# A vision layer with mixture of experts: expert loop written out, and expert results added into the normed rows by the indirect store

## The reference

```python
h = tok(x)                                   # patches @ W + b, class token, + pos_emb
h = layernorm(h + attention(h))              # 12 heads of 16, causal softmax
h = layernorm(h + moe(h))
```

```python
logits = xf @ Wg
scores, idx = top_k(logits, 2);  weights = softmax(scores)
for k in range(2):
    # position of each token in the list of its k-th expert, dropped from `capacity` on
    xg = xpad[buf]                            # (E, capacity, D)
    h = xg @ W1;  act = h[..., :H] * silu(h[..., H:])      # H = 512
    ye = act @ W2
    out = out.at[buf].add(w_buf * ye)         # dropped slots add nothing
```

## Time and profile before

| | |
|---|---|
| median of 3 runs | 2559.57 us (2555.77 to 2575.37) |
| the profiled execution | 2548.11 us |
| its span, first to last instruction | 2546.3 us |
| TensorE busy | 2192.3 us, 86% |
| DVE busy | 1640.0 us, 64% |
| POOL busy | 1389.2 us, 55% |
| ACT busy | 1105.0 us, 43% |
| mean granted TensorE clock | 0.938 |
| HBM read, written | 167.29 MB, 144.66 MB |

### The profile page before, as it was taken

The page is one execution under the profiler, slowest core; times in us unless marked ns, Lnnn a source line. Parts: engine busy times, 40 slices in busy tenths (PEclk is TensorE's granted clock), DMA queues, the critical chain, the costliest instruction groups (busy, mean ns, idle before and its releaser), DMA issues. The chain is left out here.

```text
span 2546.3 us, 50467 instructions
## 1 busy us (share of the span) xinstructions
PE 2192.3 (86%) x14772; PEld 2108.3 (83%) x14772; DVE 1640.0 (64%) x4491; ACT 1105.0 (43%) x2880; POOL 1389.2 (55%) x2562
## 2 busy tenths in 40 slices
PE   4798899999999999999989379989998999899900
PEld 3687799988989898988988379989998999899800
DVE  4366577777767677776767456656665666566556
ACT  2243344444444444444434145545454545454424
POOL 3234566665656666675756645444554545454456
PEclk8799899999999999999999789999999999999955
DMA  6889854545454454545443031101111110102187
GB/s 200 238 251 289 251 147 122 152 106 137 112 130 123 121 137 99 139 102 129 111 102 70 17 117 55 54 23 55 47 31 48 30 47 25 52 24 69 37 317 294
DMA packets 195651, 293.43 MB, mean 115 GB/s; under 512 B 43155, under 2 KB 146536, under 8 KB 190144
## 3 DMA queue, kind: packets, MB, share of 16 engines
q1 hardware_dynamic: 110480, 179.47, 25.1%
q10 hardware_dynamic: 57136, 99.73, 13.6%
q0 software_dynamic: 27904, 12.54, 2.1%
HBM read 167.29 MB, written 144.66 MB: 123 GB/s over the span
## 5 line engine op out<-in xcount | busy, mean ns | idle before, releaser
L653 PE MATMUL Y<-p,vp 128*102 128x198 f32 x1536 | 411.9, 353 | 15.9 <-POOL p L429 7.4
L140 POOL TENSOR_TENSOR e_word<-e_word 1x1 f32<-1x1 f32 x400 | 148.5, 371 | 435.2 <-DVE yout L1241 386.6
L442 POOL DMA_INDIRECT expert_lists<-pay,slot x256 | 283.1, 1106 | 58.9 <-issue 58.9
L1150 PE MATMUL Y<-w,a_hi 128*128 128x384 f32 x960 | 305.9, 357 | 10.1 <-DVE a_lo L1246 10.1
L1256 DVE TENSOR_TENSOR a<-UP,gate 128x384 f32<-128x384 f32 x320 | 178.3, 557 | 206.2 <-ACT gate L1197 205.9
L407 POOL TENSOR_TENSOR x_lo<-x,x_hi 128x396 fp32r<-128x396 f32 x192 | 212.1, 1107 | 177.8 <-ACT x_hi L462 175.9
L498 ACT ACTIVATE p<-ST 128x396 f32<-128x396 f32 x384 | 191.1, 498 | 269.2 <-PE ST L632 251.1
L1197 ACT ACTIVATE gate<-GT 128x384 f32<-128x384 f32 x320 | 157.5, 492 | 299.2 <-PE UP L1134 298.9
L1068 POOL DMA_INDIRECT expert_results<-yout,target x240 | 240.0, 1000 | 58.0 <-issue 58.0
L140 POOL TENSOR_TENSOR word_p<-word_p 1x1 f32<-1x1 f32 x416 | 90.8, 218 | 327.7 <-ACT p L500 316.3
L655 PEld LDWEIGHTS Y<-p,vp 70*102 70x102 f32 x1536 | 264.8, 173 | 1.4
(11 more groups left out here) (192 smaller groups left out, 6634.7 us busy)
## 6 DMA issues: line engine op xcount, KB each, us to landing
x<-in_xt ACTq DMA_DIRECT2D x30, 1188.0 KB
q<-qk_features SPq DMA_DIRECT2D x384, 74.2 KB, 6.4
k<-qk_features SPq DMA_DIRECT2D x192, 148.5 KB, 7.3
expert_lists<-blank ACTq DMA_DIRECT2D x16, 1455.0 KB, 9.2
rows<-expert_lists SPq DMA_DIRECT2D x80, 291.0 KB, 2.8
qk_features<-qk_hi SPq DMA_DIRECT2D x96, 198.0 KB, 2.6
qk_features<-qk_lo SPq DMA_DIRECT2D x96, 198.0 KB, 3.4
t_y<-expert_results SPq DMA_DIRECT2D x32, 576.0 KB, 7.8
```

What stands on the lines that cost most here:

```text
L140: self.eng.tensor_tensor(w[:, self.n:self.n + 1], w[:, 0:1], w[:, 0:1], ALU.add)
L442: pool.indirect_dma_start(d["lists"][:, :], bass.IndirectOffsetOnAxis(ap=slot[o][0:REAL[t], t, c:c + 1], axis=0), pay[o][0:REAL[t], t, fir ...
L653: pe.matmul(Y[0:VW1, 0:TI], v0, p32[b][:, hh, 0:TI], start=(h % 6 == 0), stop=False)
L1150: return pe.matmul(y[:, 0:2 * C], a_hi[q][:, m, c], w2[e][:, m].rearrange("p a b -> p (a b)"), start=(m == 0), stop=(m == HM - 1))
```

## The change

- The DRAM tensor `expert_results`, its eight stores of zeros and the buffer of zeros go. Both choices of a token carry the token number itself.
- The scatter adds its rows into `x1_tokens` (`compute_op=ALU.add`). Each time the list of tokens changes, every 5 chunks, POOL first waits for all scatters before it. Within a list no token occurs twice.
- The loop over four turns becomes straight code for all 80 chunks on every engine. What was done alone at the end of a turn now runs inside the next chunk, as everywhere else. Waits have constant values.
- POOL has no one-element additions in the expert block. The third scatter of a chunk moves behind `twice` of a later chunk.
- No weights are loaded, cast or split beyond the eighth expert, and `wexp` holds eight.
- The last block loads `x1_tokens` alone and adds nothing.

```diff
@@ attention_block
-                if isinstance(i, int) and i in (4, 5) and s % 3 == 1:
-                    n, rows = 4 * (i - 4) + s // 3, K2 * N // P
-                    a, b = n * rows // RESULTS, (n + 1) * rows // RESULTS
-                    act.dma_start(d["y"].rearrange("(p t) c -> p t c", p=P)[:, a:b, :],
-                                  repeat(zeros[:], b - a)).then_inc(s_yclear, 16)
...
-                        ch.mark(dve.tensor_scalar(pb[:, :, 1], tid[:], float(N), None, ALU.add))
+                        ch.mark(dve.tensor_copy(pb[:, :, 1], tid[:]))
@@ expert_block, gpsimd
-            def scatter(it, cc, t):
+            def scatter(cc, t):
 
                 n = 3 * cc + t
-                words.wait((s_yout, it * (3 * NC2) + (n + 1)))
-                q = 3 * (cc % 2) + t
+                q = n % 6
+                if t == 0 and cc and cc % (CPE // 2) == 0:
+
+                    for b in range(6):
+                        pool.wait_ge(s_out[b], 16 * ((n - 1 - b) // 6 + 1))
+                pool.wait_ge(s_yout, n + 1)
                 pool.indirect_dma_start(
-                    d["y"][:, :], bass.IndirectOffsetOnAxis(ap=target[cc % 4][:, t:t + 1], axis=0),
-                    yout[q][:], None, bounds_check=K2 * N - 1, oob_is_err=False)\
+                    d["x1"][:, :], bass.IndirectOffsetOnAxis(ap=target[cc % 4][:, t:t + 1], axis=0),
+                    yout[q][:], None, bounds_check=N - 1, oob_is_err=False, compute_op=ALU.add)\
                     .then_inc(s_out[q], 16)
...
-            with loop(pool, 0, E // 2) as it:
-                columns_twice(it, 0)
-                for cc in range(NC2):
-                    if cc + 1 < NC2:
-                        columns_twice(it, cc + 1)
...
+            columns_twice(0)
+            for cc in range(NCH):
+                if cc + 1 < NCH:
+                    columns_twice(cc + 1)
+                if cc >= 2:
+                    scatter(cc - 2, 2)
+                x, j = cc // CPE + 1, cc % CPE
+                if x < E:
                     if j == 0:
 
-                        pool.wait_ge(s_raw[e], (it + (1 if e else 2)) * 16)
-
-                    words.wait((s_ug, it * (4 * NC2) + 4 * cc))
-                    src, hi, _ = parts(j, e)
+                        pool.wait_ge(s_raw[x % 2], (x // 2 + 1) * 16)
+
+                    wait(pool, s_ug, 4 * cc)
+                    src, hi, _ = parts(j, x % 2)
                     pool.tensor_copy(hi, src).then_inc(s_whi, 1)
-                    if cc:
-                        for t in range(3):
-                            scatter(it, cc - 1, t)
-                for t in range(3):
-                    scatter(it, NC2 - 1, t)
+                if cc:
+                    for t in range(2):
+                        scatter(cc - 1, t)
+            scatter(NCH - 2, 2)
+            for t in range(3):
+                scatter(NCH - 1, t)
@@ expert_block, tensor
-            with loop(pe, 0, E // 2) as it:
-                turn_rows(it, 0)
-                for cc in range(NC2):
-                    for m in range(HM):
-                        first(it, cc, m)
-                        if cc and m:
-                            second(it, cc - 1, m - 1)
-                        if m == 1 and cc + 1 < NC2:
-                            turn_rows(it, cc + 1)
-                for t in range(3):
-                    second(it, NC2 - 1, t)
+            turn_rows(0)
+            for cc in range(NCH):
+                for m in range(HM):
+                    first(cc, m)
+                    if cc and m:
+                        second(cc - 1, m - 1)
+                    if m == 1 and cc + 1 < NCH:
+                        turn_rows(cc + 1)
+            for t in range(3):
+                second(NCH - 1, t)
@@ last_block
-                for dst, v, ap, f in ((a, x_v, d["x1"], 0), (y0, y0_v, d["y"], 0), (y1, y1_v, d["y"], N)):
-                    src = v[c] if rows == P else rest(ap, f)
-                    sp.dma_start(dst[q][0:rows, 0:t, :], src).then_inc(s_in[q], 16)
+                src = x_v[c] if rows == P else rest(d["x1"], 0)
+                sp.dma_start(a[q][0:rows, 0:t, :], src).then_inc(s_in[q], 16)
...
-                pool.wait_ge(s_in[q], (turn + 1) * 48)
-                pool.tensor_tensor(a[q][0:rows, 0:t], a[q][0:rows, 0:t], y0[q][0:rows, 0:t],
-                                   ALU.add).then_inc(s_sum, 1)
...
-                dve.wait_ge(s_sum, c + 1)
-                dve.tensor_tensor(a[q][0:rows, 0:t], a[q][0:rows, 0:t], y1[q][0:rows, 0:t],
-                                  ALU.add).then_inc(s_all, 1)
-                dve.wait_ge(s_all, c + 1)
+                dve.wait_ge(s_in[q], (turn + 1) * 16)
```

More of the change, by code:

```diff
@@ L1037, in _ @@
             chunk_rows = d["lists"].rearrange("(n p t) c -> n p t c", p=P, t=3)
-            with loop(sp, 0, E // 2) as it:
-                for cc in range(NC2):
-                    if cc < 2:
-                        sp.wait_ge(s_split, it * NC2 + cc if cc else it * NC2)
-                    else:
-                        sp.wait_ge(s_split, it * NC2 + (cc - 1))
-                    sp.dma_start(rows[cc % 2][:], chunk_rows[it * NC2 + cc])\
-                        .then_inc(s_rows[cc % 2], 16)
-                    if cc % CPE == 2:
-                        e = cc // CPE
-                        sp.wait_ge(s_wlo, it * 20 + 10 * (e + 1))
-                        sp.dma_start(raw[e][:], d["wexp"][it * 2 + (e + 2)]).then_inc(s_raw[e], 16)
+            for cc in range(NCH):
+                wait(sp, s_split, cc - 1)
+                sp.dma_start(rows[cc % 2][:], chunk_rows[cc]).then_inc(s_rows[cc % 2], 16)
+                x = cc // CPE
+                if cc % CPE == 2 and x + 2 < E:
+                    sp.wait_ge(s_wlo, 10 * (x + 1))
+                    sp.dma_start(raw[x % 2][:], d["wexp"][x + 2]).then_inc(s_raw[x % 2], 16)
         @block.gpsimd
         def _(pool):
-            pool.memset(word_p[:], 0.0).then_inc(s_word, 1)
-            pool.wait_ge(s_word, 1)
-            words = Words(pool, word_p)
             pool.wait_ge(s_raw[0], 16)
@@ L1174, in _, with rows_hi @@
+            for cc in range(NCH):
+                for m in range(HM):
[6 more added lines that the diff above has]
+                second(NCH - 1, t)
         @block.scalar
         def _(act):
-            def rows_hi(it, cc):
-                act.wait_ge(s_xt, it * NC2 + (cc + 1))
+            def rows_hi(cc):
+                act.wait_ge(s_xt, cc + 1)
@@ L1190, in hidden_hi @@
                 act.activation(a_hi[cc % 2][:, m], a32[m % 2][:], ACT.Copy).then_inc(s_ahi, 1)
-            with loop(act, 0, E // 2) as it:
-                rows_hi(it, 0)
-                for cc in range(NC2):
-                    for m in range(HM):
-                        act.wait_ge(s_ug, it * (4 * NC2) + (4 * cc + m + 1))
-                        act.activation(gate[m % 2][:], GT[m % 2][:, 0:TILE3], ACT.Silu).then_inc(s_gate, 1)
-                        if cc and m:
-                            y_lo(it, cc - 1, m - 1)
-                        if m:
-                            hidden_hi(it, cc, m - 1)
-                        if m == 1 and cc + 1 < NC2:
-                            rows_hi(it, cc + 1)
-                    hidden_hi(it, cc, HM - 1)
-                for t in range(3):
-                    y_lo(it, NC2 - 1, t)
+            rows_hi(0)
@@ new lines, in _ @@
+            for cc in range(NCH):
+                for m in range(HM):
+                    act.wait_ge(s_ug, 4 * cc + m + 1)
+                    act.activation(gate[m % 2][:], GT[m % 2][:, 0:TILE3], ACT.Silu).then_inc(s_gate, 1)
+                    if cc and m:
+                        y_lo(cc - 1, m - 1)
+                    if m:
+                        hidden_hi(cc, m - 1)
+                    if m == 1 and cc + 1 < NCH:
+                        rows_hi(cc + 1)
+                hidden_hi(cc, HM - 1)
@@ L1208, in _ @@
+            for t in range(3):
+                y_lo(NCH - 1, t)
         @block.vector
@@ L1233, in rows_lo, with y_out @@
                                   ALU.subtract).then_inc(s_split, 1)
-            def y_out(it, cc, t):
+            def y_out(cc, t):
                 n, q = 3 * cc + t, 3 * (cc % 2) + t
-                dve.wait_ge(s_ylo, it * (3 * NC2) + (n + 1))
-                dve.wait_ge(s_out[q], it * (NC2 // 2 * 16) + 16 * (cc // 2)) if cc >= 2 else \
-                    dve.wait_ge(s_out[q], it * (NC2 // 2 * 16))
+                dve.wait_ge(s_ylo, n + 1)
+                wait(dve, s_out[q], 16 * (cc // 2))
@@ new lines, in _ @@
+            for cc in range(NCH):
+                x = cc // CPE + 1
+                for m in range(HM):
+                    wait(dve, s_alo, 4 * cc + m - 1)
+                    dve.wait_ge(s_gate, 4 * cc + m + 1)
+                    dve.tensor_tensor(a32[m % 2][:], UP[m % 2][:, 0:TILE3], gate[m % 2][:], ALU.mult)\
+                        .then_inc(s_a, 1)
+                    if cc and m:
```

(12 more changed lines are left out.)

109 lines of the change are left out of this document (37 added, 72 removed).

## The result

| | before | after |
|---|---|---|
| median | 2558.66 us (2555.77 to 2575.37) | 2451.06 us (2449.86 to 2454.87) |
| the profiled execution | 2548.11 us | 2454.87 us |
| its span | 2546.3 us | 2453.1 us |
| mean granted TensorE clock | 0.938 | 0.95 |
| HBM read, written | 167.29, 144.66 MB | 145.04, 125.29 MB |

The changed kernel takes 0.9547 of the time before (95% interval 0.951 to 0.9584), 107.6 us less by the medians. One execution of experiment 3 fell in a slower state, 3076.04 us at a mean clock of 0.65, and the median given there leaves it out. In later measurements the kernel before lies higher, at medians of 2570.68, 2575.19 and 2571.03 us; beside the last of these the changed kernel has 2449.19 (experiment 9), 121.8 us less.

A forecast was written before the change was run, and what follows sets the result against it. TensorE was taken to bound the attention and expert stages, with DMA 84% busy in the last block. Savings 24 + 29 - 1 + 47 = 99 us gave 2449 from the profiled run, 2461 from the median; forecast 2458, range 2436 to 2493.

The forecast's parts named there:

- Part 1: Attention stage: without zero stores two slow bodies run like their neighbours, 24 us saved (14 to 25.4).
- Part 2: Expert stage: written-out loop turns three joints into plain expert changes, chunks stay 11.00 us; 29 us saved (24 to 34.5).
- Part 3: POOL in the expert stage: earlier `twice` costs nothing; adding store takes 1.0 to 1.5 us, lands after 3 to 4.
- The limit of 3.1 without gaps: Expert stage: three adding stores fit into an 11.00 us chunk up to 3.1 us each on POOL.
- Part 4: Expert stage: POOL's waits at 15 list changes cost nothing unless a store lands after more than about 11 us.
- End of the stage: Expert stage's end: nothing hides the last store's landing, 1 us more (0 to 4.6).
- Part 5: Last block: one load instead of three, no additions; 75 us instead of 122.3, 47 saved (33 to 52).
- circle of loads: Last block: a load waits for ACT four chunks back; landing, statistics and ACT total 10.2 us, 3.4 a chunk.
- A: Rival, expert stage: adding store makes POOL the bound, slower; 240 us per further us above 3.1; chance 0.10.
- B: Rival, expert stage: late landings make POOL's waits reach TensorE modestly, 2488 or 2533 us; chance 0.07.
- C: Rival, attention stage: bodies keep their pace because something other than zeros slows them, 2482 us; chance 0.08.
- D: Rival, last block: gains little if the load-store mix is slower, 4.5 us a chunk, 2473 us; chance 0.08.

The follow-up runs named there:

- experiment 3: Changed kernel, still written out, but chunks 20, 40 and 60 ordered as at the old loop's joints; 2474.93 us, ratio 0.9626.
- experiment 9: The changed kernel measured again, unaltered, as base for later runs; 2449.19 us, ratio 0.9541.
- Experiment 1: Kernel before without the eight stores of zeros, its last block loading the normed rows three times; 2543.63 us, ratio 0.9895.
- experiment 4: Changed kernel with the indirect store writing instead of adding; 2453.32 us, ratio 0.9537.
- experiments 5 and 6: Changed kernel with each adding store issued twice (2554.17 us, ratio 0.9918) and three times (2989.05 us, ratio 1.1607), the further ones into unread tensors.
- experiment 10: Changed kernel with POOL waiting for all earlier stores before every store, 239 waits instead of 15; 2567.28 us, ratio 0.9981.
- Experiment 12: Changed kernel with the tenth weight piece split earlier and DVE scaling two of six rows in the last block; 2421.79 us, ratio 0.9417.
- experiment 6: Changed kernel with each adding store issued three times, the further two into unread tensors; 2989.05 us, ratio 1.1607.
- experiment 8: Changed kernel with both additions back in the last block, on resident zero tiles without their loads; 2499.24 us, ratio 0.9705.

## Why the prediction was right, and where it was not

The total was 7 us off (2458 said, 2451 measured), and the signs of all terms were right. The gain was 101 by the medians as said and 107.6 as measured, 121.8 in the later pair: Parts 2 and 5 were taken too small, by 4 and 8 us.

**Part 1, zero stores: 24 us, right by the medians.** Taking them out or putting them back moves the median by 27 and 25. The two profiled executions show 6.2 only, because one had the clock at 1.00 in bodies 6 to 9 and the other at 0.92, which is chance: the twelve executions without the stores have 164.3 to 177.5 us there. The reason given was right in part. The two bodies lose 20 us (some 21 in the mean of the twelve) and not 25, and their `shift` starts are 43.4 and 44.1 us apart and not 41, with the clock at 0.92, which the lower end of 14 had allowed for. No row places the other 5 us or so of the medians, so that 24 fits so well is partly luck. The prediction set its sum against one execution of before that was itself 10.6 us lucky; it saw that and moved from 2449 to 2458, which was too much by the result.

**Part 2, loop written out: 29 said, 33.0 measured.** The base of 77 x 11.00 was exact. The seven expert changes were put at the mean of 2.33 and 3.83, 21.6 in all; they cost 17.8, as five lay at the short end; that is the whole difference. The gain does not all come from the changes of expert, though: 1.3 us of the 33.0, counted in the 29 without a cause, are of one other chunk. At 2359.52 in before, with no joint near, TensorE had waited 1.11 us for `twice`, which stood behind a late scatter:

```profile
2357.83 0.98 POOL L1068 DMA_INDIRECT expert_results<-yout,target  x1 [2.83 <-issue]
...
2358.97 0.49 POOL L1078 COPY twice<-rows 128x384 f32<-128x384 f32 x1
```

That chunk took 12.33 us; it is 11.00 now that `twice` goes first (Part 3). Experiment 1, which keeps the old order, has it too. The cause named was also the right one: experiment 3 brings 31.4 us back with the order alone.

**Part 3, the store: inside what was tolerated, outside what was taken.** 1.57 us against 1.0 to 1.5, and 1.85 with its gap; landing 2.7 (8.1 at the longest) against 3 to 4. Neither moves a chunk, as experiment 4 shows. The limit of 3.1 without gaps holds: with a gap of 0.30 it is 3.4 by experiments 5 and 6.

**Part 4, waits: cost nothing, as said, but for an incomplete reason.** In twelve of the 15 places the first store of the list is held back by 0.1 us and in three by 0.8 to 0.9, and nothing of TensorE's is behind it. What the argument lacked is the 0.8 us between an event and the start of the store that waits for it; at 15 places it is hidden, at 239 (experiment 10) it is part of the 3.5 us and more a store that cost 118 us.

**End of the stage:** 1 said, 0.9 measured.

**Part 5, last block: 75 said, 68.05 measured; the mechanism right, three terms too long.** The head is 8.0 and not 10.9, and the trace of before had the greater reason already. Its own first load landed after 3.8 us, as the one of after did after 3.70, where 5.8 had been carried over from loads with others in flight. And from the first statistics to ACT it took 4.2 (2388.86 to 2393.08), not 5.1, as POOL's power `t_rstd` fell too; here of before and of after, with the load of before ahead of them:

```profile
t_x<-x_tokens SPq DMA_DIRECT2D x1, 576.0 KB, 3.8
...
2438.21 2.41 POOL L1338 TENSOR_TENSOR t_rstd<-t_var,t_half 128x6 f32<-128x6 f32 x1 [0.72 <-DVE t_var L1379]
...
2391.48 1.37 POOL L1312 TENSOR_TENSOR t_rstd<-t_var,t_half 128x6 f32<-128x6 f32 x1 [6.10 <-DVE t_var L1347]
```

The pace is 3.40 and not 3.6: ACT's 2.74 and gaps of 0.66 in the mean, 0.42 between the first ones, against the 0.74 of the earlier trace rows. By the chain ACT sets it and not the circle of loads, but the circle is close behind. Experiment 12 brings 6.8 us by moving ACT's work, which agrees; it is no proof, since ACT's work is a part of the circle too. The tail is 5.7 and not 6.6.

The estimate worked out from the Trainium skill, page DMA: Bandwidth & Descriptors, section Anatomy of one DMA, was 3.35 us for that load and 71 for the block: nearer than the 5.8, though 0.35 under the measured 3.70; the loads in flight together took 5.0. The page fits this for a DMA that GpSimd issues, and these are issued by SyncE. `t_shift` fell to 0.15, as both the row and the page had it.

**The rivals.** A and B: the store is neither long nor late enough; A's mechanism is real (experiment 6). C: the two bodies did lose their 20 us, so it fell, although the pair of profiles looks like it. D: the mix was not slower, 3.40 a chunk.

Open stays why TensorE's clock falls to 0.50 once a body in some executions and not in others of the same kernel; no run here was made to tell. Open stays too why the medians of experiment 3 show 22 to 24 us of the 31 that its stretch shows.

## What to carry to other kernels

Writing a pipelined loop out pays through what the joint did to the order (here 31.4 us came back with the order alone, of 33.0), so ask which work stands alone at the end of a turn; whether the same gain can be had without unrolling all, no run here tried. When two causes hold a stage at nearly the same level (loads at 104.5, additions at about 110), removing one alone shows little of what removing both gives. A store that must wait for the one before it costs its landing and 0.8 to 1.0 us more each time, so keep such waits to the places where targets can really repeat; and compare medians before two single profiles are subtracted.

## What the runs showed of the hardware

- An indirect store of 128 rows of 768 bytes that adds takes POOL 1.57 us and lands after 2.7, against 0.99 and 2.1 for the plain one; back to back it takes 1.85.
- From the end of what it waits for to the start of an indirect store pass about 0.8 us (0.78 in after, 0.8 to 1.0 behind a landing in experiment 10). A store waiting for the one before starts 3.5 us after it at the earliest, 4.2 in the mean.
- `t_shift` of DVE and `t_rstd` of POOL, both of 128x6, take 0.15 and 1.32 us in after and 1.80 and 2.15 in experiment 8, where the other engine adds tiles of 128x1152 beside them.
- The first transpose of the expert stage moved by 24 us between profiled kernels without zero stores, whose attention stages are the same but for one small DVE instruction; the clock in bodies 6 to 9 was 0.92 in after and 0.99 in experiment 9: a noise of 1% in a single profile.
- The last block with three loads a chunk moved 372 GB/s over its 104 us, where before it had 318 with the additions beside them.
